# A fused convolution and sparse-expert block: moving small selection work, and transposing by image half

## The chip, the cores and the metric

The kernel runs on one core of one Trainium2 chip, in one launch. The time is device microseconds of that core; each value quoted for a kernel is the median of several runs. A separate execution is profiled and gives the trace.

## The reference

```python
x = x + conv_block(ln_c(x))     # ln_c: layer norm over the 64 channels of a pixel
t = to_tokens(x)                # [8, 16384, 64]
t = t + experts(ln_t(t))        # ln_t: layer norm of a token
x = from_tokens(t)

def conv_block(x):              # x: [8, 64, 128, 128] fp32
    xn = groupnorm(x, 8 groups) * gn_w + gn_b
    h = relu(w1 @ xn + b1)                      # 1x1 convolutions, 64 -> 64
    return x + w2 @ h + b2

def experts(x):                 # 32 experts, each takes its 8 best tokens of 16384
    logits = x @ gate_w.T + gate_b
    vals, idx = top_k(softmax(logits, over tokens), 8)
    pooled = sum over k of x[idx_k] * vals_k
    out = w2[e] @ [gelu(w1[e] @ [pooled, 1]), 1]
    return scatter_add(idx, out * vals)
```

## The kernel before

A batch (image) lies in SBUF as 128 partitions (two image halves of 64 channels) by 8192 pixels. It is cut into eight units `u` of 1024 columns. Two batches are resident (`xs`, `us`, two buffers each).

Iteration `it` works on three batches at once. For batch `b = it` it runs the convolutions, unit by unit: `conv1` (L350, TensorE), `relu` (L622, ScalarE), `conv2` (L361, TensorE), and `x1` (L784, VectorE), which adds `xs`, to which POOL has already added the normalized input (`add`, L1129). The next unit's `conv1` writes the banks `cv` that `x1` has just read. From the finished unit come `tokens` (transposes, copied by ScalarE in `token_copy` and stored by SP in `store`), `logits` (copied in `logits_copy`), and sums and sums of squares for the tokens' layer norm. For batch `n = it + 1` it computes the channel layer norm: sums (`x_sums`), `mean`, centering ("C" jobs), squares and their sums (`xc_square_sums`), `rstd`, scaling ("S" jobs with a group-norm sum). For batch `t = it - 1` it scales the logits ("L" jobs) and takes the top 8 of each of four pieces of 2048 positions (`top`, L848: a maximum and an index search over 1024 columns each), with an exponential and its sum on ScalarE (`explog`).

The pieces' winners become 32 candidates a row (`candidates`, L857), which one matrix product brings together ("M" job); `merge_pixels` and `merge_values` (L870, L892) take the final eight from them in many operations of a few hundred columns or fewer, with two small exponentials on ScalarE between (`merge_exps`, L682). This merge is for batch `m = it - 2`, in slots 2 and 3.

Everything is ordered by hand. Each engine runs its own queue in program order; a "slot" `s` is unit `s` of an iteration, and the dictionaries at L46 to L59 say at which place `(s, 0)` to `(s, 3)` of a slot a job stands. A job is: TensorE spreads 32-row statistics over 128 partitions into the two banks `bc` (`spread_stat`, L412), then VectorE uses them (`use_spread`, L760), then the banks are free for the next one. Unit 0 of each batch is done in `boundary`, together with the group norm (`group_norm`, L807), the last unit's tokens and the layer norm of the finished batch (`ln2_variance`, L833, `ln2_rstd`, L839). `boundary` also holds the top 8 of the fourth piece and the candidates. POOL's adds of units 6 and 7 wait for the group norm's bias.

In the last iteration there is no next batch; `spread_pixels` (L515), `diagonals` and `equal_pixels` compare the chosen pixel numbers of two batches, a pair in each of slots 5, 6 and 7, and `token_norm` normalizes the gathered rows. Then come the last batch's selection, the experts, and 16 indirect scatters.

The eight PSUM banks are `bc` (2), `cv` (2), `pt` (tokens), `lgp` (logits), `st1` and `st2` (sums).

Of the kernel before, what the change touches and what calls it, by code (L numbers as in the profile page):

```python
# [8 lines left out]
ALU = mybir.AluOpType  # L9
# [13 lines left out]
NCH = 2 * NU  # L23
# [26 lines left out]
M_JOB, LAST_M_JOB = (2, 3), (5, 0)  # L50


SUMSQ_AT = {(2, 1): (0,), (3, 0): (1,), (4, 0): (2,), (4, 1): (3,)}
# [3 lines left out]
TOP_AT = {3: 0, 5: 1, 6: 2}  # L57
LAST_TOP_AT = {1: 0, 2: 1, 3: 2, 4: 3}
LATE_ADDS = (6, 7)  # L59
PAIR_AT, NORM_AT = (5, 6, 7), (5, 6, 7)  # L60


def jobs_of(it):

    p1, tl, m = it + 1 < NB, 1 <= it <= NB, it - 2
    jobs = {}
    if p1:
        jobs.update({at: ("C", k) for at, k in C_JOBS.items()})
        jobs.update({at: ("S", k) for at, k in S_JOBS.items()})
    if tl:  # L70
        jobs.update({at: ("L", k) for at, k in (L_JOBS if p1 else LAST_L_JOBS).items()})
    if 0 <= m < NB - 2:
        jobs[M_JOB] = ("M", m)
    if it >= NB - 1:
        jobs[LAST_M_JOB] = ("M", it - 1)
    return jobs
# [9 lines left out]
def mk_metaformer_kernel(nc, x, gn_w, gn_b, w1T, b1, w2T, b2, gateT, gate_b, e_w1, e_w2, *outs):  # L86
    ctx = ExitStack()
    with ctx:
# [100 lines left out]
        pt, lgp, st1, st2 = banks("pt"), banks("lgp"), banks("st1"), banks("st2")  # L189
# [91 lines left out]
        def _(sp):  # L281
# [34 lines left out]
            def store(b, u):  # L316
                sp.wait_ge(tok_done, NCH * b + 2 * u + 2)
# [21 lines left out]
        def _(pe):  # L339
# [72 lines left out]
            def spread_stat(it, at):  # L412
# [18 lines left out]
                if kind == "M":  # L431
                    pe.wait_ge(cnd4_ready, k + 1)
                    pe.matmul(mrg_p, fold[:].rearrange("p g e -> p (g e)"), cnd4[:].rearrange("p r c -> p (r c)"),
# [15 lines left out]
            def boundary(it, par):  # L449
# [17 lines left out]
                if last >= 0:  # L467
                    x1_square_sums(last, NG - 1)
# [8 lines left out]
            def iteration(it, par, p1, p2):  # L477
                b, n = it, it + 1
                for s in range(0 if not p2 else 1, NU):
                    if p2:  # L480
                        conv1(b, par, s)
                        tokens(b, par, s - 1, 0)
                    spread_stat(it, (s, 0))
                    if p2:
                        logits(b, par, s - 1)
# [7 lines left out]
                    spread_stat(it, (s, 1))  # L493
                    if p2 and not p1 and s in PAIR_AT:
                        spread_pixels(PAIR_AT.index(s))
                    if p2:
                        conv2(b, s)
                        tokens(b, par, s - 1, 1)
                    spread_stat(it, (s, 2))
                    if p1:  # L500
                        for m in SUMSQ_AT.get((s, 1), ()):
# [13 lines left out]
            def spread_pixels(p):  # L515

                pe.wait_ge(diag_ready, p + 1)
                pe.wait_ge(bc_used, job_count(7, "M", 6) if p < 3 else job_count(8, "M", 7))
# [23 lines left out]
            pe.wait_ge(tok_done, NCH * NB)  # L542
# [67 lines left out]
        def _(act):  # L610
# [18 lines left out]
            def token_copy(b, u, sl):  # L629
                j = NCH * b + 2 * u + sl  # L630
                act.wait_ge(t_done, j + 1)
                wait(act, stored[u % 2], 16 * ((NU * b + u) // 2))
                nc.scalar.activation(tok[u % 2][:, :, 4 * sl:4 * sl + 4].rearrange("p h t c -> p t h c"),  # L633
                                     pt[:].rearrange("p (t h c) -> p t h c", t=4, h=2), ACT.Copy).then_inc(tok_done, 1)

            def logits_copy(b, u):
# [6 lines left out]
                nc.scalar.activation(lg[:, col:col + CH], lgp[:], ACT.Copy).then_inc(lcopy_done, 1)  # L643
# [44 lines left out]
            def boundary(it, par):  # L688
# [5 lines left out]
                if last >= 0:  # L694
                    token_copy(last, NU - 1, 0)
                    square_x1(last, 1 - par, NU - 1)
                    logits_copy(last, NU - 1)
                    token_copy(last, NU - 1, 1)
                if b < NB:
                    relu(b, par, 0)  # L700
                if last >= 0:
                    ln2_mean_square(last)
                    ln2_rsqrt(last)
                if 0 <= m < NB - 2:
                    explog(m, PIECES - 1)

            def iteration(it, par, p1, p2):
                b, n, t, m = it, it + 1, it - 1, it - 2
                tops = TOP_AT if p1 else LAST_TOP_AT
                for s in range(0 if not p2 else 1, NU):  # L710
                    if p2:
                        relu(b, par, s)
                        token_copy(b, s - 1, 0)
                    square_stat(it, (s, 0))
                    if p2:
                        logits_copy(b, s - 1)
                    square_stat(it, (s, 1))
                    if p2:
                        token_copy(b, s - 1, 1)
                        square_x1(b, par, s - 1)  # L720
                    square_stat(it, (s, 2))
                    if p1 and s == 4:
# [4 lines left out]
                        nc.scalar.activation(y0[:], lnv[:], ACT.Exp, scale=-0.5).then_inc(y0_ready, 1)  # L727
                    square_stat(it, (s, 3))
                    if t >= 0 and s in tops:
                        explog(t, tops[s])  # L730
                    if s == 3 and 0 <= m < NB - 2:
                        merge_exps(m)
                    if it == NB - 1 and s == 6:
                        merge_exps(t)
# [24 lines left out]
        def _(dve):  # L759
# [88 lines left out]
            def top(t, i):  # L848
# [4 lines left out]
                link(nc.vector.max(cnd[:, K * i:K * i + K], piece(t, i)))  # L853
                link(nc.vector.max_index(top_i[:, K * i:K * i + K], cnd[:, K * i:K * i + K], piece(t, i)))  # L854
# [335 lines left out]
```

## Time and profile before

| | |
|---|---|
| median of 3 runs | 765.37 us (764.79 to 770.71) |
| the profiled execution | 758.62 us, span 756.9 us |
| mean granted TensorE clock | 0.901 |
| TensorE matmul busy | 568.5 us, 75% |
| VectorE busy | 494.7 us, 65% |
| ScalarE busy | 428.0 us, 57% |
| GpSimd (POOL) busy | 185.1 us, 24% |

Busy time is how long an engine had an instruction in work, matmuls by a modelled end, so it is not a share of peak. The granted clock is a share of 2.4 GHz; it has two levels, 1.2 and 2.4 GHz. The span runs from the first to the last instruction. In the trace rows below, an "idle before" with a name in square brackets is how long the engine waited and for which instruction; PEld is TensorE's loading of weights. One row stands for several like instructions in a row (x4, x8, x16); a start is that of the first.

### The profile page before, as it was taken

The page shows a single profiled execution, that of the slowest core. Times are in us where ns is not written, and L with a number is a line of the kernel's source. Part 1 is how long each engine was busy: PE and PEld are TensorE (multiplying, and loading weights), DVE is VectorE, ACT ScalarE, POOL GpSimd, SP SyncE. Part 2 cuts the span into 40 slices and gives each one's busy share as a digit, 9 for nine tenths or more (in the row PEclk, how much of TensorE's full clock was granted, in tenths as well). Part 3 has the DMA queues.
Part 4 walks back from the last instruction along what each step waited for, and adds up shares of the span by engine and source line. Part 5 has one row for each costly group of instructions (what it writes and reads, how often), then busy time and mean ns, then how long its engine had stood idle before and what let it go on. Part 6 is the DMA issues. An engine that isn't in the chain of part 4 may idle for free.

```text
span 756.9 us, 14016 instructions
## 1 busy us (share of the span) xinstructions
PE 568.5 (75%) x5630; PEld 285.5 (38%) x5630; DVE 494.7 (65%) x919; ACT 428.0 (57%) x658; POOL 185.1 (24%) x110
## 2 busy tenths in 40 slices
PE   2544998898788878887888788878987867651682
PEld 0212344444344334443444344434443323230382
DVE  2344456668688768876887677778776876468320
ACT  0234587677857685768576856685768464222200
POOL 1026007203320332033204320342033700010025
PEclk9999999999999999999999999899999899775555
DMA  9930044634334333333333333333111295010000
GB/s 204 178 68 1 29 140 119 182 106 126 112 112 113 112 112 113 112 112 112 113 112 113 112 112 113 112 113 112 57 56 57 75 206 133 29 59 0 4 8 22
DMA packets 35428, 73.38 MB, mean 97 GB/s; under 512 B 12292, under 2 KB 14372, under 8 KB 31268
## 3 DMA queue, kind: packets, MB, share of 16 engines
q1 hardware_dynamic: 34340, 71.44, 34.6%
q0 software_dynamic: 1024, 1.05, 0.6%
q8 instruction: 45, 0.74, 0.4%
q14 instruction: 19, 0.16, 0.1%
HBM read 38.40 MB, written 34.08 MB: 96 GB/s over the span
## 4 chain that ended last, share of the span: by engine, by line
PE 42%; DVE 32%; issue 14%; ACT 6%; DMA 2%; POOL 1%; SPq 1%; ACTq 0%; DVEq 0%; POOLq 0%
PE st L346 9%; DVE xs L788 7%; PE bc L445 7%; PE lgp L383 6%; DVE top_i L854 6%; PE pt L373 5%; DVE cnd L853 5%; PE cv L357 5%; PE cv L365 4%; DVE us L778 3%; DVE us L780 3%; ACT hid L627 2%; DMA xs<-in_x 2%; ACT junk L666 2%; DVE lg L776 2%
## 5 line engine op out<-in xcount | busy, mean ns | idle before, releaser
L1135 POOL TENSOR_TENSOR xs<-xs,us 128x1024 f32<-128x1024 f32 x64 | 150.3, 2370 | 438.1 <-DVE gsum L780 354.9
L659 ACT ACTIVATE sqc<-us 128x1024 f32<-128x1024 f32 x64 | 67.5, 1054 | 78.9 <-DVE us L778 74.0
L373 PEld LDWEIGHTS pt<-ident,xs 128*128 128x128 f32 x512 | 68.6, 196 | 101.9 <-issue 100.5
L788 DVE SCALAR_TENSOR_TENSOR xs<-cv,vecs,xs 128x1024 f32<-128x1024 f32 x64 | 81.9, 1280 | 35.2 <-PE cv L365 35.0
L778 DVE TENSOR_TENSOR us<-xs,bc 128x1024 f32<-128x1024 f32 x64 | 77.9, 1217 | 39.6 <-PE bc L445 39.6
L633 ACT ACTIVATE tok<-pt 128x512 f32<-128x512 f32 x128 | 75.4, 589 | 47.6 <-PE pt L373 47.5
L445 PE MATMUL bc<-rstd_s,spread 32*128 32x256 f32 x384 | 54.2, 363 | 58.0 <-DVE gsum L780 32.1
L780 DVE CUSTOM_DVE_ANT_0 us<-us,bc 128x1024 f32<-128x1024 f32 x64 | 77.9, 1217 | 29.4 <-PE bc L445 29.4
L373 PE MATMUL pt<-ident,xs 128*128 128x128 f32 x512 | 94.7, 310 | 1.0 <-DVE xs L788 0.8
L346 PE MATMUL st<-xs,stat_w 128*32 128x256 f32 x1024 | 76.2, 426 | 16.1 <-DMA xs<-in_x 16.1
L666 ACT ACTIVATE junk<-us 128x1024 bf16<-128x1024 f32 x64 | 67.6, 1056 | 30.6 <-DVE gsum L780 30.6
L357 PE MATMUL cv<-us,w1n 64*64 64x512 f32 x512 | 72.1, 634 | 16.6 <-DVE xs L788 16.6
L627 ACT ACTIVATE hid<-cv,b1n 128x1024 f32<-128x1024 f32 x64 | 70.7, 1105 | 22.8 <-PE cv L357 22.2
L365 PE MATMUL cv<-hid,w2bd 64*64 64x512 f32 x512 | 72.7, 639 | 12.6 <-ACT hid L627 12.6
L383 PE MATMUL lgp<-xs,gcen 128*32 128x256 f32 x1024 | 76.3, 420 | 0.0
L648 ACT ACTIVATE sqx<-xs 128x1024 f32<-128x1024 f32 x64 | 67.3, 1051 | 0.0
L445 PEld LDWEIGHTS bc<-rstd_s,spread 32*128 32x128 f32 x384 | 32.9, 210 | 86.2 <-DVE gsum L780 41.4
L671 ACT ACTIVATE lg<-lg,nmax 128x1024 f32<-128x1024 f32 x32 | 36.6, 1145 | 50.0 <-DVE nmax L855 50.0
L346 PEld LDWEIGHTS st<-xs,stat_w 128*32 128x32 f32 x1024 | 34.4, 121 | 51.1 <-issue 24.3
L776 DVE TENSOR_TENSOR lg<-lg,bc 128x1024 f32<-128x1024 f32 x32 | 39.0, 1218 | 13.9 <-PE bc L445 12.6
L445 PE MATMUL bc<-mean_s,spread 32*128 32x256 f32 x256 | 34.7, 351 | 17.1 <-DVE mean_s L795 10.5
L346 PE MATMUL st<-sqc,stat_w 128*32 128x256 f32 x512 | 41.2, 448 | 1.8 <-ACT sqc L659 1.8
(181 smaller groups left out, 609.0 us busy)
## 6 DMA issues: line engine op xcount, KB each, us to landing
xs<-in_x SPq DMA_DIRECT2D x64, 512.0 KB, 6.4
out_rows<-tok SPq DMA_DIRECT2D x64, 512.0 KB, 2.8
us<-in_e_w SPq DMA_DIRECT2D x4, 520.0 KB
xs<-in_e_w SPq DMA_DIRECT2D x8, 256.0 KB
sqc<-out_rows,idx_all POOLq DMA_INDIRECT x16, 2.5
out_rows<-sqc,idx_all POOLq DMA_INDIRECT x16, 2.1
vecs<-in_b SPq DMA_DIRECT2D x4, 0.2 KB, 13.1
gate_bias<-in_gate_b SPq DMA_DIRECT2D x4, 0.1 KB, 11.4
```

What stands on the lines that cost most here:

```text
L346: mm = pe.matmul(dst[32 * c:32 * c + 32], stat_w[:, q, :], src[:, col:col + SUB], start=first and m == 0 and sub == 0, stop=True, skip_gro ...
L357: mm = pe.matmul(cv[C * sl:C * sl + C, CH * h:CH * h + CH], w1n[par][r, r], half_chunk(us[par], u, h, sl), start=True, stop=True)
L365: mm = pe.matmul(cv[C * h:C * h + C, CH * sl:CH * sl + CH], w2bd[r, r], hid[r, CH * h:CH * h + CH], start=True, stop=True)
L373: mm = pe.transpose(pt[:, P * k:P * k + P], unit(xs[par], u)[:, 4 * sl + k:UN:8], ident[:])
L383: mm = pe.matmul(lgp[NE * c:NE * c + NE, SUB * sl:SUB * sl + SUB], gcen[:, NE * h:NE * h + NE], xs[par][:, col:col + SUB], start=True, sto ...
L445: mm = pe.matmul(bc[:, CH * sl + SUB * i:CH * sl + SUB * i + SUB], weights, stat[32 * c:32 * c + 32, :], start=True, stop=True)
L627: nc.scalar.activation(hid[:], cv[:], ACT.Relu, bias=b1n[:, par:par + 1]).then_inc(h_done, 1)
L666: nc.scalar.activation(junk[:], unit(us[n % 2], k), ACT.Square, accum_out=gsq[:, k:k + 1]).then_inc(usq_done, 1)
L778: ins = nc.vector.tensor_tensor(unit(us[n % 2], k), unit(xs[n % 2], k), bc[:], ALU.subtract)
L780: ins = nc.vector.tensor_tensor_reduce(unit(us[n % 2], k), unit(us[n % 2], k), bc[:], 1.0, 0.0, ALU.mult, ALU.add, gsum[:, k:k + 1])
L788: nc.vector.scalar_tensor_tensor(out=xu, in0=cv[:], scalar=vecs[:, 3:4], in1=xu, op0=ALU.add, op1=ALU.add).then_inc(x1_done, 1)
L1135: nc.gpsimd.tensor_tensor(xu, xu, su, ALU.add).then_inc(s_done, 1)
```

## The change

Five things change together.

1. The selection of batch `t` runs in one iteration: maxima at `(s, 0)` in slots 2, 3, 5, 6, index searches behind `x1` of the same slots, candidates in slot 7, the M job at `(7, 2)`, and the merge's small operations in the following `boundary`, in place of the fourth piece's `top`.
2. The transposes of a unit are 16 of 64 partitions by a 64x64 identity instead of 8 of 128 partitions. The first half's go to one bank and the second half's to the other, in one group ahead of the first spread; one ScalarE copy of 128x1024 takes both. The first bank is also that of the logits, so `logits` moves behind the token copy and `conv2`.
3. Sums of squares move: all stand ahead of `conv2` but the first. ScalarE squares x1 and copies the logits later in the slot.
4. `ln2_variance` writes its intermediate to PSUM, not to SBUF.
5. POOL's adds of units 6 and 7 wait for `x1` of unit 1.

The last iteration is rearranged alike (pairs in slots 4, 5, 6).

```diff
-SUMSQ_AT = {(2, 1): (0,), (3, 0): (1,), (4, 0): (2,), (4, 1): (3,)}
+SUMSQ_AT = {(2, 2): (0,), (3, 0): (1,), (4, 0): (2,), (4, 1): (3,)}
-M_JOB, LAST_M_JOB = (2, 3), (5, 0)
+M_JOB, LAST_M_JOB = (7, 2), (6, 2)
-TOP_AT = {3: 0, 5: 1, 6: 2}
-LAST_TOP_AT = {1: 0, 2: 1, 3: 2, 4: 3}
+TOP_AT = {2: 0, 3: 1, 5: 2, 6: 3}
+LAST_TOP_AT = {2: 0, 3: 1, 4: 2, 5: 3}
-PAIR_AT, NORM_AT = (5, 6, 7), (5, 6, 7)
+PAIR_AT, NORM_AT = (4, 5, 6), (4, 5, 6)
...
-        pt, lgp, st1, st2 = banks("pt"), banks("lgp"), banks("st1"), banks("st2")
+        tl, st1, st2 = banks("tl", 2), banks("st1"), banks("st2")
+        lgp, pt = tl[:, 0:CH], tl[:, CH:2 * CH]
...
-            def tokens(b, par, u, sl):
+            def tokens(b, par, u):
                 pe.wait_ge(x1_done, NU * b + u + 1)
-                wait(pe, tok_done, NCH * b + 2 * u + sl)
-                for k in range(4):
-                    mm = pe.transpose(pt[:, P * k:P * k + P], unit(xs[par], u)[:, 4 * sl + k:UN:8], ident[:])
+                wait(pe, tok_done, NU * b + u)
+                wait(pe, lcopy_done, NU * b + u)
+                for k in range(8):
+                    for h in range(HALVES):
+                        r = slice(C * h, C * h + C)
+                        mm = pe.transpose(tl[:, CH * h + C * k:CH * h + C * k + C], unit(xs[par], u)[r, k:UN:8], ident[r, r])
                 mm.then_inc(t_done, 1)
...
             def logits(b, par, u):
-                pe.wait_ge(x1_done, NU * b + u + 1)
-                wait(pe, lcopy_done, NU * b + u)
+                pe.wait_ge(tok_done, NU * b + u + 1)
...
# TensorE, a slot
                     if p2:
                         conv1(b, par, s)
-                        tokens(b, par, s - 1, 0)
+                        tokens(b, par, s - 1)
                     spread_stat(it, (s, 0))
-                    if p2:
-                        logits(b, par, s - 1)
...
                     spread_stat(it, (s, 1))
+                    if p1:
+                        for m in SUMSQ_AT.get((s, 1), ()):
+                            xc_square_sums(n, m)
...
                         conv2(b, s)
-                        tokens(b, par, s - 1, 1)
+                        logits(b, par, s - 1)
                     spread_stat(it, (s, 2))
...
# TensorE, boundary
-                    tokens(last, 1 - par, NU - 1, 0)
-                    logits(last, 1 - par, NU - 1)
+                    tokens(last, 1 - par, NU - 1)
                     x1_sums(last, 1 - par, NG - 1)
-                    tokens(last, 1 - par, NU - 1, 1)
...
                     conv1(b, par, 0)
                 if last >= 0:
+                    logits(last, 1 - par, NU - 1)
                     x1_square_sums(last, NG - 1)
...
# ScalarE, a slot
                         relu(b, par, s)
-                        token_copy(b, s - 1, 0)
+                    if t >= 0 and s - 1 in tops:
+                        explog(t, tops[s - 1])
+                    if p2:
+                        token_copy(b, s - 1)
                     square_stat(it, (s, 0))
-                    if p2:
-                        logits_copy(b, s - 1)
                     square_stat(it, (s, 1))
...
+                    if p2:
+                        square_x1(b, par, s - 1)
+                        logits_copy(b, s - 1)
                     square_stat(it, (s, 2))
...
# VectorE, boundary
-                if 0 <= m < NB - 2:
-                    top(m, PIECES - 1)
+                if m >= 0:
+                    link3 = merge_pixels(it - 1, m)
                 if last >= 0:
                     link2 = Steps(dve, ln2_steps, LN2_STEPS * last)
                     ln2_variance(last, link2)
...
                     ln2_rstd(last, link2)
-                if 0 <= m < NB - 2:
-                    candidates(m)
+                if m >= 0:
+                    merge_values(m, link3)
# VectorE, a slot
                     use_spread(it, (s, 0))
+                    if t >= 0 and s in tops:
+                        top_values(t, tops[s])
+                    if t >= 0 and s == (7 if p1 else 6):
+                        candidates(t)
                     use_spread(it, (s, 1))
                     if p2:
                         x1(b, par, s)
-                    use_spread(it, (s, 2))
                     if p1 and s == 1:
                         mean(n)
                     if p1 and s == 4:
                         rstd(n)
...
+                    use_spread(it, (s, 2))
+                    if t >= 0 and s in tops:
+                        top_places(t, tops[s])
                     use_spread(it, (s, 3))
...
# ln2_variance
-                link(nc.vector.scalar_tensor_tensor(out=v2[:], in0=st2[:, SUB:2 * SUB], scalar=EPS, in1=ta[:],
+                link(nc.vector.scalar_tensor_tensor(out=st2[:, SUB:2 * SUB], in0=st2[:, SUB:2 * SUB], scalar=EPS, in1=ta[:],
                                                     op0=ALU.add, op1=ALU.subtract))
-                nc.vector.tensor_scalar(v2[:], v2[:], EPS, None, ALU.max).then_inc(var2_ready, 1)
+                nc.vector.tensor_scalar(v2[:], st2[:, SUB:2 * SUB], EPS, None, ALU.max).then_inc(var2_ready, 1)
# POOL, units 6 and 7
-                    pool.wait_ge(w1n_ready, 2 * (n + 1))
+                    pool.wait_ge(x1_done, NU * n + 2)
```

## Rows read from the trace of the kernel before

**Rows 1.** Windows: stretch, length, busy us of five engines, clock, DMA share, GB/s.
```profile
142.59:213.15 70.56, 60.73 (x668) 29.85 (x660) 53.09 (x81) 50.63 (x77) 18.82 (x8) 0.98 0.42 120
213.15:288.32 75.17, 62.88 (x667) 30.65 (x662) 57.87 (x103) 52.55 (x81) 18.82 (x8) 0.95 0.40 113
...
592.31:661.84 69.53, 49.88 (x399) 20.61 (x400) 45.15 (x97) 31.80 (x51) 11.51 (x12) 0.85 0.49 113
```

**Rows 2.** Timeline of TensorE in slot 3: start, us, operation.
```profile
231.32 1.09 PE L357 MATMUL cv<-us,w1n 64*64 64x512 f32 x8
232.34 0.71 PE L373 MATMUL pt<-ident,xs 128*128 128x128 f32 x4
232.98 0.50 PE L445 MATMUL bc<-mean_s,spread 32*128 32x256 f32 x4
233.41 1.07 PE L383 MATMUL lgp<-xs,gcen 128*32 128x256 f32 x16
234.30 1.05 PE L346 MATMUL st<-sqx,stat_w 128*32 128x256 f32 x16
235.16 1.05 PE L346 MATMUL st<-sqc,stat_w 128*32 128x256 f32 x16
...
236.57 1.09 PE L365 MATMUL cv<-hid,w2bd 64*64 64x512 f32 x8
...
239.16 1.09 PE L357 MATMUL cv<-us,w1n 64*64 64x512 f32 x8 [0.43 <-DVE xs L788]
```

**Rows 3.** The same timeline: `conv1` of the other slots, and the group-norm product.
```profile
214.47 1.09 PE L357 MATMUL cv<-us,w1n 64*64 64x512 f32 x8 [0.67 <-DVE xs L788]
...
222.56 1.09 PE L357 MATMUL cv<-us,w1n 64*64 64x512 f32 x8
...
251.61 1.12 PE L357 MATMUL cv<-us,w1n 64*64 64x512 f32 x8
...
259.76 1.09 PE L357 MATMUL cv<-us,w1n 64*64 64x512 f32 x8
...
268.58 1.09 PE L357 MATMUL cv<-us,w1n 64*64 64x512 f32 x8 [0.34 <-DVE xs L788]
...
277.89 0.38 PE L457 MATMUL bc<-gs,gsel 128*128 128x2 f32 x2 [1.51 <-DVE gs L812]
...
289.65 1.09 PE L357 MATMUL cv<-us,w1n 64*64 64x512 f32 x8 [0.67 <-DVE xs L788]
```

**Rows 4.** The same timeline: the stalled spread of slot 4.
```profile
246.61 0.51 PE L445 MATMUL bc<-rstd_s,spread 32*128 32x256 f32 x4 [2.56 <-DVE us L778]
```

**Rows 5.** Timeline of VectorE in slot 4: an operation of `merge_values`.
```profile
244.59 0.17 DVE L895 TENSOR_TENSOR djunk<-dexp,mrg 128x16 f32<-128x16 f32 x1 [1.71 <-ACT dexp L685]
```

**Rows 6.** Groups by line: busy us, mean ns of one, idle before them and its releasers.
```profile
L788 DVE SCALAR_TENSOR_TENSOR xs<-cv,vecs,xs 128x1024 f32<-128x1024 f32 x64 | 81.9, 1280 | 35.2 <-PE cv L365 35.0
L778 DVE TENSOR_TENSOR us<-xs,bc 128x1024 f32<-128x1024 f32 x64 | 77.9, 1217 | 39.6 <-PE bc L445 39.6
L633 ACT ACTIVATE tok<-pt 128x512 f32<-128x512 f32 x128 | 75.4, 589 | 47.6 <-PE pt L373 47.5
L627 ACT ACTIVATE hid<-cv,b1n 128x1024 f32<-128x1024 f32 x64 | 70.7, 1105 | 22.8 <-PE cv L357 22.2
L373 PEld LDWEIGHTS pt<-ident,xs 128*128 128x128 f32 x512 | 68.6, 196 | 101.9 <-issue 100.5 <-DVE xs L788 1.0
L853 DVE MAX8 cnd<-lg 128x8 f32<-128x1024 f32 x32 | 39.2, 1224 | 0.1
L671 ACT ACTIVATE lg<-lg,nmax 128x1024 f32<-128x1024 f32 x32 | 36.6, 1145 | 50.0 <-DVE nmax L855 50.0
```

**Rows 7.** Timeline of TensorE in the last iteration: the pixel products of slots 5 and 6.
```profile
634.91 1.12 PE L520 MATMUL bc<-xs,gsel 128*128 128x512 f32 x2
...
645.79 2.07 PE L520 MATMUL bc<-xs,gsel 128*128 128x512 f32 x2 [3.73 <-DVE xs L985]
```

**Rows 8.** Line 837, the variance's clamp: ns of one, least/median/most; first and last start.
```profile
L837 DVE TENSOR_SCALAR lnv<-lnv x8: 295/1966/2329, 140.5 to 668.4; 128x256 f32<-128x256 f32 x8
```

More of the change, by code:

```diff
@@ L432, in spread_stat @@
                     pe.wait_ge(cnd4_ready, k + 1)
+                    if it == NB - 1:
+                        pe.wait_ge(eq_ready, 3)
                     pe.matmul(mrg_p, fold[:].rearrange("p g e -> p (g e)"), cnd4[:].rearrange("p r c -> p (r c)"),
@@ L497, in iteration @@
                         conv2(b, s)
-                        tokens(b, par, s - 1, 1)
+                        logits(b, par, s - 1)
                     spread_stat(it, (s, 2))
                     if p1:
-                        for m in SUMSQ_AT.get((s, 1), ()):
+                        for m in SUMSQ_AT.get((s, 2), ()):
                             xc_square_sums(n, m)
@@ L541, in _ @@
             pe.wait_ge(ew_in, 16 * 13)
-            pe.wait_ge(tok_done, NCH * NB)
+            pe.wait_ge(tok_done, NU * NB)
             for h in range(HALVES):
@@ L694, in boundary @@
                 if last >= 0:
-                    token_copy(last, NU - 1, 0)
+                    token_copy(last, NU - 1)
                     square_x1(last, 1 - par, NU - 1)
-                    logits_copy(last, NU - 1)
-                    token_copy(last, NU - 1, 1)
                 if b < NB:
@@ L701, in boundary @@
                 if last >= 0:
+                    logits_copy(last, NU - 1)
                     ln2_mean_square(last)
                     ln2_rsqrt(last)
-                if 0 <= m < NB - 2:
-                    explog(m, PIECES - 1)
+                if m >= 0:
+                    merge_exps(m)
             def iteration(it, par, p1, p2):
@@ L727, in iteration @@
                         nc.scalar.activation(y0[:], lnv[:], ACT.Exp, scale=-0.5).then_inc(y0_ready, 1)
+                    if p2:
+                        square_x1(b, par, s - 1)
+                        logits_copy(b, s - 1)
+                    square_stat(it, (s, 2))
                     square_stat(it, (s, 3))
[L729 to L734, printed above, removed]
                     if p2 and not p1 and s == NORM_AT[1]:
@@ L846, in ln2_rstd, with top_values @@
                 assert link.n == LN2_STEPS, link.n
-            def top(t, i):
+            def top_values(t, i):
                 link = Steps(dve, top_steps, TOP_STEPS * t + 2 * i)
@@ L930, in iteration @@
                         rstd(n)
-                    use_spread(it, (s, 3))
-                    if t >= 0 and s in tops:
-                        top(t, tops[s])
-                    if s == 2 and 0 <= m < NB - 2:
-                        link3 = merge_pixels(it, m)
-                    if s == 3 and 0 <= m < NB - 2:
-                        merge_values(m, link3)
+                    if not p1 and s in PAIR_AT:
+                        equal_pixels(PAIR_AT.index(s))
+                    use_spread(it, (s, 2))
+                    if t >= 0 and s in tops:
+                        top_places(t, tops[s])
+                    use_spread(it, (s, 3))
                     if p2 and not p1:
@@ L940, in iteration @@
                             nc.vector.memset(ones[:], 1.0)
-                        if s == 4:
-                            candidates(t)
-                        if s == 5:
-                            link3 = merge_pixels(it, t)
-                        if s == 6:
-                            merge_values(t, link3)
                         if s in NORM_AT:
                             token_norm(0, 0, 6, (NORM_AT.index(s),))
-                        if s in PAIR_AT:
-                            equal_pixels(PAIR_AT.index(s))
                         if s + 1 in PAIR_AT:
@@ L1048, in _ @@
             for i in range(PIECES):
-                top(7, i)
+                top_values(7, i)
+                top_places(7, i)
             candidates(7)
```

30 lines of the change are left out of this document (11 added, 19 removed).

## The prediction

> **What bounds the kernel now.** I cut the run into stretches from one batch's first `x1` to the next [rows 1]. Five steady iterations, 213.15 to 592.31, take 75.8 us each; in the one that starts at 213.15 VectorE is busy 57.9, ScalarE 52.6 and TensorE 62.9 us (a span that is not its peak), so no engine is full and waits set the pace. The iteration before it, which has no merge, no late fourth piece and no candidates, took 70.56 us: the small selection work costs about 5 us where it stands.
>
> TensorE's timeline tells where. In slot 3 its groups follow one another without a gap [rows 2], so their spacing is their price: `conv1` 1.02, four transposes 0.64, a spread 0.43, `logits` 0.89, a sum group 0.86, `conv2` 1.02 us. From one `conv1` to the next, slots 1 to 6 last 8.09, 8.76, 7.84, 12.45, 8.15 and 8.82 us; from the last `conv1` to the group-norm product 9.31, and from there to the next iteration's second `conv1` 11.76 (214.47 to 289.65, 75.18 in all) [rows 2, 3]. The outlier is slot 4: the spread at 246.61 stood idle for 2.56 us, for VectorE's subtraction that should have freed the `bc` banks. VectorE had queued a whole top-8 (maximum and index search) and the end of a merge ahead of it, and the merge waited another 1.71 us for ScalarE, whose small exponentials sat behind the 1.15 us one [rows 4 to 6]. Behind that stall TensorE lost its clock (0.95 of full speed on average over the iteration [rows 1]), which makes slot 4 longer still.
>
> **The change, part by part.** Let t be the time of a unit's sixteen transposes. I walk a steady iteration in each engine's new order, with durations of one instruction [rows 2, 6] and 0.1 us for a hand-over between engines. These sums are estimates.
>
> *Transposes.* Two groups of four cost 2 x 0.64 = 1.28 us. Now 16 instructions load 64x128 and stream 64 columns. Four of the old ones, each loading 128 and streaming 128 columns, take 0.64, so 0.16 each, and with half the streaming 0.12 if loading and streaming weigh alike. If the two row halves run side by side, t is 8 x 0.12 = 0.96; one after the other, 16 x 0.12 = 1.92. Lower end, if only the streamed columns count and halves overlap: 8 x 0.08 = 0.64. I take 0.95, because other packed tiles overlap here: `conv1` streams eight times 512 columns in 1.02 us in quarters of the array [rows 2], a full-array product of twice 512 columns takes 1.12 [rows 7]. ScalarE's copy of 128x1024 should cost what its PSUM-read ReLU of that shape costs, 1.10, against 2 x 0.59 before [rows 6]: nothing won. The banks are the hidden price: transposes of a unit now also wait for the copy of the previous unit's logits, and logits for the token copy.
>
> *Slots 2 and 3.* The order is `conv1`, transposes, spread, VectorE job, maximum, job, `x1`, next `conv1`: 1.02 + t + 0.43 + 1.22 + 1.22 + 1.22 + 1.28 and hand-overs of about 0.1 = 6.5 + t = 7.45 us each. Index searches fall after `x1`, beside TensorE work, and the merge is gone: gains of 1.3 and 0.4.
>
> *Slot 4.* No piece is searched and no merge stands here, but the last sum of squares now precedes `conv2` and needs the seventh square, which ScalarE reaches after ReLU, exponential and copy, at 6.5 us (its queue is 2.2 us late from slot 3: 2.2 + 1.1 + 1.2 + 1.0 + 1.0). Then sum 0.9, `conv2` 1.0, `logits` 0.9, spread 0.45: 9.8, a gain of 2.65, and TensorE stands idle 1.7 us.
>
> *Slots 5 and 6.* VectorE enters slot 5 with the reciprocal root and a logits job, 3.15 us; then maximum, job, `x1`, job, about 1.25 each, and the last spread 0.5: 8.65 (a loss of 0.5). Slot 6: ScalarE's ReLU begins at 3.3, behind the third square; ReLU, exponential and copy end at 6.6, then `logits` and a spread: 8.0 (gain 0.8).
>
> *Slot 7.* Transposes wait for the logits copy until 2.35; S6, the candidates with their wait for the last exponential (5.75), S7, `x1`, the merge's two copies and the last square bring the group-norm product to 9.7 (loss 0.4). The POOL queue's two late adds now start behind the second `x1`, and are needed five slots later: nothing; its gathers, queued behind them, find their indices earlier. SP's store waits for one copy of a unit instead of two, no later than before: nothing.
>
> *Boundary.* The whole old top-8 goes, 14 small operations of the merge come at about 0.2 us each, some 2.8 us either way, and both lie beside TensorE's own chain to `conv2`: product 0.4, t with a 0.4 wait, sums 0.9, bias product 0.2, `conv1` 1.0, `logits` 0.9, three sum groups 2.7 make 7.5 us to `conv2`, and 2.5 to the next `conv1`; the old way took 11.76 with a throttled stretch in it, so I add 1.0: 10.95 (gain 0.8). The clamp of the variance lasted 1.97 us at the median and 0.295 at the least, where POOL was quiet [rows 8]; with a PSUM source I give it 0.42, but in the sum above `conv2`, not the clamp, sets the start of `x1`: I count 0.3.
>
> A rule bears on that. The Trainium skill ("SBUF — State Buffer", Who interferes with whom) says that VectorE in a two-port mode and GpSimd take a shared port pair in turn, each blocking the other wholly. By it the clamp gives back 1.55 us seven times, 11 us, if it set the end; the trace agrees with the 1.97 against 0.295, but not that the end waits for it.
>
> *Slot 1.* `mean` now precedes the second logits job and waits for the last sum of x, which stands behind `logits`: the first spread of the next batch moves from 4.6 to 5.0 us behind `conv2`. With the merge's last four operations inside `ln2`'s shadow: 8.4 (loss 0.3).
>
> Sum: 8.4 + 7.45 + 7.45 + 9.8 + 8.65 + 8.0 + 9.7 + 10.95 = 70.4 against 75.2. I add 1.4 for one more stretch at the lower clock: 71.8. Over five iterations 5 x 71.8 = 359 against 379.2: -20.2. The 70.56 one gains the work it lacked: +1.2. The first iteration has no selection: 0.
>
> *The last iteration* took 69.5 us from `x1` to `x1` [rows 1]. If its four slots without a pixel product take 8.2 us each, like the steady ones, the three with one take 12.2 each. There `conv2` waits behind the product, which waits for VectorE's diagonals: 3.73 us idle at 645.79 [rows 7]. The merge leaves these slots (2.8 us and a tail of four operations, 0.8) and index searches (1.5) stay in two of them. From `x1` through equality, search, normalization and diagonals to the next product, `conv2` and `x1` I count 9.8, 9.8 and, without a following pair, 7.5: -9.5; the merge product's wait for the third equality gives back 1: -8.5. The rest, 95 us, keeps its chain: 0.
>
> Total -27.5 us. The profiled execution took 758.62 us (span 756.9); the median of the runs is 765.37, 6.75 above. So 731 by the profiled one, and 738 by the median, which I forecast.
>
> **The rivals.**
> *Slower: the row halves do not overlap.* Then t = 1.92, one us more, in about six places of eight iterations: +48, so 738 + 48 = 786. It turns the gain into a loss when t passes 0.95 + 27.5/48 = 1.5. Against it: the quarters of `conv1` [rows 2]. For it: nothing in this trace shows a transpose in a tile.
> The Trainium skill ("TensorE: Matmul & The Clock Gate", LDWEIGHTS) has load time go by columns, not by rows. The trace agrees, 196 ns for 128x128 [rows 6]: by it sixteen loads of half the rows cost sixteen full loads.
>
> *The gain goes to new waits and the clock.* The walk leaves TensorE idle 2.2 us in slot 1, 1.7 in slot 4 and 2.0 in slot 5; 2.56 us of idling went before a slower clock in the old slot 4. If each is followed by a stretch like it, 1.6 us apiece, an iteration is 75 us: 738 + 6 x 3.2 = 757; range 748 to 764.
>
> *A larger gain.* If the long stall's end keeps the clock at its upper level and t is 0.64, an iteration is 68.5: 738 - 20 = 718.
>
> *It does nothing*, since the bound is TensorE's own work: the gapless slot 3 speaks for it, slot 4 against it: 765.
>
> **How the numbers follow.** Forecast 730 to 748: 0.50. New waits and clock: 0.23. Larger gain: 0.11. Slower: 0.11. Nothing: 0.05. Less than 1% (7.7 us) can't be told from no change. Faster takes the forecast, the larger gain and nearly two thirds of the second case: 0.75; same: the rest of that and the last: 0.14; slower 0.11. The range leaves out most of the slower case and the far end of the larger gain: 720 to 765.
>
> **What would show it.** Right: a unit's 16 transposes span about 1 us; from `x1` to `x1` of two batches 70 to 73 us; the slot-4 spread has no 2.6 us gap and TensorE waits instead for ScalarE's square; the clamp takes 0.4 us; last iteration near 61. Wrong: transposes at 1.5 us or more; gaps of 2 us in slots 1 and 5 with a granted clock below 0.93; ScalarE's token copies waited for by `logits` in most slots.

## The result, and the profile after

The changed kernel takes 742.26 us (median of four runs, 740.17 to 742.73); the kernel before took 765.08 beside it (762.92 to 770.71). The ratio is 0.9686, interval 0.9631 to 0.9741: 22.8 us less. The forecast was 738. Some executions of a kernel are slower as a whole, at a lower granted clock; the ratios leave them out, and the profile of `old_clamp` below is of such a one.

The profiled execution took 742.05 us, span 740.3. The windows from `x1` to `x1`, columns as in [rows 1]: a steady iteration, the last one, and the first.

```profile
363.75:435.42 71.67, 62.32 (x730) 29.73 (x729) 56.00 (x102) 51.51 (x73) 18.78 (x8) 0.93 0.43 119
...
578.90:644.67 65.77, 46.48 (x444) 18.64 (x448) 40.14 (x71) 30.79 (x41) 16.20 (x14) 0.84 0.52 120
79.50:146.81 67.31, 59.19 (x712) 27.73 (x710) 35.23 (x55) 47.21 (x63) 18.77 (x8) 0.95 0.41 116
```

The five steady iterations took 359.65 us together instead of 379.16, 3.9 less on the average. In the one shown TensorE is busy 0.6 us less than in the second row of [rows 1] and VectorE 1.9, 1.55 of it in the clamp: most of the 3.5 us between these two is waits. The last iteration lost 3.8 us, the first grew by 3.6, and the second, 70.56 us before, took 72.44.

TensorE's timeline in slots 3 and 4, answering to [rows 2] and [rows 4]:

```profile
382.45 1.09 PE L355 MATMUL cv<-us,w1n 64*64 64x512 f32 x8
383.47 1.10 PE L374 MATMUL tl<-ident,xs 64*128 64x64 f32 x16
384.50 0.50 PE L447 MATMUL bc<-mean_s,spread 32*128 32x256 f32 x4
...
396.17 1.07 PE L344 MATMUL st<-sqc,stat_w 128*32 128x256 f32 x16 [1.01 <-ACT sqc L659]
```

Sixteen transposes occupy 383.47 to 384.50, 1.03 us, where two groups of four took 1.28. The stalled spread is gone, and TensorE waits in slot 4 for ScalarE's square instead.

In the boundary, VectorE's timeline shows small operations of the merge at their bare length, and then idle time before `x1`; the last row answers to the clamp of [rows 8]:

```profile
430.52 0.17 DVE L875 CAST best<-fpos 128x8 f32<-128x8 uint32 x1
430.73 0.16 DVE L876 TENSOR_TENSOR gbm<-best,gate_bias 128x1 f32<-128x1 f32 x1
...
433.56 0.42 DVE L831 TENSOR_SCALAR lnv<-st 128x256 f32<-128x256 f32 x1
435.42 1.28 DVE L782 SCALAR_TENSOR_TENSOR xs<-cv,vecs,xs 128x1024 f32<-128x1024 f32 x1 [1.44 <-PE cv L363]
```

One thing that the prediction has nowhere stands in slot 3 of the last iteration. TensorE first, then ScalarE, VectorE, POOL. Where a bracket has `issue` or `remote`, the profile names no instruction that ended the wait:

```profile
593.88 1.10 PE L374 MATMUL tl<-ident,xs 64*128 64x64 f32 x16
594.91 1.07 PE L344 MATMUL st<-sqx,stat_w 128*32 128x256 f32 x16
595.91 1.09 PE L363 MATMUL cv<-hid,w2bd 64*64 64x512 f32 x8
599.94 1.51 PE L383 MATMUL tl<-xs,gcen 128*32 128x256 f32 x13 [2.95 <-ACT tok L634]
...
608.86 1.99 PE L355 MATMUL cv<-us,w1n 64*64 64x512 f32 x8 [6.09 <-DVE xs L782]
```
```profile
598.87 1.02 ACT L634 ACTIVATE tok<-tl 128x1024 f32<-128x1024 f32 x1 [2.61 <-remote]
606.05 1.06 ACT L648 ACTIVATE sqx<-xs 128x1024 f32<-128x1024 f32 x1 [6.17 <-remote]
...
607.52 1.28 DVE L782 SCALAR_TENSOR_TENSOR xs<-cv,vecs,xs 128x1024 f32<-128x1024 f32 x1 [12.10 <-issue]
...
590.35 1.12 POOL L1118 DMA_INDIRECT sqc<-out_rows,idx_all  x1 [0.17 <-issue]
...
604.26 0.95 POOL L1118 DMA_INDIRECT sqc<-out_rows,idx_all  x1 [0.30 <-issue]
```

The transposes end by 595 and the copy that waits for them starts at 598.87; `conv2` ends by 597 and `x1` starts at 607.52, which had nothing else to wait for. By TensorE's records the work is done, and the news of it comes 4 to 11 us late, while POOL issues twelve gathers (590.35 to 605.2). Slot 3 takes 16.0 us.

### The profile page after: what moved, and what is told of

The parts are those of the page before. It is cut to its first block, busy times and chain, and to the rows that moved or that the text cites. A ratio compares the mean times of both kernels' runs of the same rounds, so it can differ in the third digit from the quotient of the medians.

```text
span 740.3 us, 14809 instructions
## 1 busy us (share of the span) xinstructions
PE 564.1 (76%) x6142; PEld 276.7 (37%) x6142; DVE 480.8 (65%) x919; ACT 422.0 (57%) x594; POOL 184.8 (25%) x110
## 4 chain that ended last, share of the span: by engine, by line
PE 42%; DVE 27%; issue 15%; ACT 11%; DMA 3%; POOL 1%; SPq 1%; ACTq 0%; another core or an unknown queue 0%; DVEq 0%; POOLq 0%
PE st L344 11%; PE bc L447 6%; PE tl L374 6%; DVE us L774 6%; PE cv L355 6%; DVE xs L782 5%; PE cv L363 4%; PE tl L383 3%; DVE cnd L847 3%; DVE lg L770 3%; DVE us L772 2%; DMA xs<-in_x 2%; DVE top_i L852 2%; ACT lg L671 2%; ACT sqc L659 2%
## 5 line engine op out<-in xcount | busy, mean ns | idle before, releaser
L772 DVE TENSOR_TENSOR us<-xs,bc 128x1024 f32<-128x1024 f32 x64 | 78.1, 1221 | 40.2 <-PE bc L447 39.7
L629 ACT ACTIVATE hid<-cv,b1n 128x1024 f32<-128x1024 f32 x64 | 70.8, 1106 | 53.9 <-PE cv L355 53.9
L344 PE MATMUL st<-xs,stat_w 128*32 128x256 f32 x1024 | 86.4, 472 | 16.8 <-DMA xs<-in_x 16.8
L355 PE MATMUL cv<-us,w1n 64*64 64x512 f32 x512 | 76.1, 667 | 13.7 <-DVE xs L782 12.4
L374 PEld LDWEIGHTS tl<-ident,xs 64*128 64x128 f32 x1024 | 62.1, 201 | 64.6 <-issue 63.3
L374 PE MATMUL tl<-ident,xs 64*128 64x64 f32 x1024 | 71.1, 287 | 15.3 <-ACT lg L643 15.2
L383 PE MATMUL tl<-xs,gcen 128*32 128x256 f32 x1024 | 73.0, 401 | 5.3 <-ACT tok L634 4.9
L634 ACT ACTIVATE tok<-tl 128x1024 f32<-128x1024 f32 x64 | 64.9, 1015 | 7.4 <-PE tl L374 4.8
L383 PEld LDWEIGHTS tl<-xs,gcen 128*32 128x32 f32 x1024 | 27.9, 112 | 74.3 <-issue 38.7
L447 PE MATMUL bc<-mean_s,spread 32*128 32x256 f32 x256 | 36.4, 365 | 23.1 <-DVE lg L770 13.7
L344 PEld LDWEIGHTS st<-xs,stat_w 128*32 128x32 f32 x1024 | 32.2, 127 | 52.8 <-issue 29.0
L643 ACT ACTIVATE lg<-tl 128x512 f32<-128x512 f32 x64 | 37.5, 585 | 18.9 <-PE tl L383 18.4
```

What stands on the lines that cost most here:

```text
L344: mm = pe.matmul(dst[32 * c:32 * c + 32], stat_w[:, q, :], src[:, col:col + SUB], start=first and m == 0 and sub == 0, stop=True, skip_gro ...
L355: mm = pe.matmul(cv[C * sl:C * sl + C, CH * h:CH * h + CH], w1n[par][r, r], half_chunk(us[par], u, h, sl), start=True, stop=True)
L374: mm = pe.transpose(tl[:, CH * h + C * k:CH * h + C * k + C], unit(xs[par], u)[r, k:UN:8], ident[r, r])
L383: mm = pe.matmul(lgp[NE * c:NE * c + NE, SUB * sl:SUB * sl + SUB], gcen[:, NE * h:NE * h + NE], xs[par][:, col:col + SUB], start=True, sto ...
L447: mm = pe.matmul(bc[:, CH * sl + SUB * i:CH * sl + SUB * i + SUB], weights, stat[32 * c:32 * c + 32, :], start=True, stop=True)
L629: nc.scalar.activation(hid[:], cv[:], ACT.Relu, bias=b1n[:, par:par + 1]).then_inc(h_done, 1)
```

## The experiments

All ratios are to the kernel before, run on the same chip. Its median was 756.0 us beside `sel_only`, `tok_only`, `full128` and `serial_halves`, 760.2 beside `after_again`, `weights_late`, `sumsq_late` and `old_clamp`, and 756.3 beside the other four, so times of different groups are compared by ratio. The edits are shown against the changed kernel; `...` marks lines left out.

**One half of the change each.** `sel_only` keeps the old transposes and banks, and has all the rest of the change, parts 3 to 5 too:

```diff
-        tl, st1, st2 = banks("tl", 2), banks("st1"), banks("st2")
+        pt, lgp, st1, st2 = banks("pt"), banks("lgp"), banks("st1"), banks("st2")
...
-                        tokens(b, par, s - 1)
+                        tokens(b, par, s - 1, 0)
                     spread_stat(it, (s, 0))
+                    if p2:
+                        logits(b, par, s - 1)
```

> The kernel before with the selection work spread as in the changed kernel, and the transposes, their two copies and the banks as they were. Theory A (the selection work carries the gain): the long wait of slot 4 and the merge leave the iteration, a steady iteration takes 72 to 73 us from x1 to x1 against 75.8, the whole about 746 (ratio 0.975). Rival B (the transposes and the one copy carry it): 758 or more, a steady iteration 75 us. Rival C (the parts need each other): 765 or above.

`tok_only` has the new transposes, banks, copy and place of `logits`, and the selection work, the other sums of squares, the clamp and the wait of the late adds as they were:

```diff
-M_JOB, LAST_M_JOB = (7, 2), (6, 2)
+M_JOB, LAST_M_JOB = (2, 3), (5, 0)
...
-TOP_AT = {2: 0, 3: 1, 5: 2, 6: 3}
+TOP_AT = {3: 0, 5: 1, 6: 2}
```

> The kernel before with the transposes per row half into two banks with one copy, and logits behind conv2; the selection work stays where it was. Theory A: 1.28 us of transposes a unit become 1.05, everything else of slot 4's wait stays: a steady iteration 74.5 to 76 us, the whole 757 to 766. Rival B: 745 or less. Rival C (the bank chain transposes, token copy, logits, logits copy alone makes it slower): above 772.

Measured: `sel_only` 728.56 us, 0.9616 (0.9572 to 0.9661); `tok_only` 765.12, 1.0132 (1.0082 to 1.0183). A window of each, and a row of TensorE's timeline of `tok_only`:

```profile
286.71:358.45 71.74, 63.76 (x666) 30.93 (x665) 55.63 (x103) 52.07 (x83) 18.83 (x8) 0.93 0.42 118
```
```profile
289.37:364.27 74.90, 61.78 (x730) 29.26 (x729) 57.26 (x103) 52.17 (x74) 18.85 (x8) 0.95 0.41 113
364.27:445.19 80.92, 68.57 (x730) 30.97 (x729) 56.78 (x102) 53.13 (x74) 18.81 (x8) 0.85 0.38 105
```
```profile
322.79 0.51 PE L447 MATMUL bc<-rstd_s,spread 32*128 32x256 f32 x4 [2.77 <-DVE us L772]
```

For `sel_only` theory A holds, and more: the change without its transposes carries the whole gain (0.9616 where 0.975 was expected). How much of that is the moved selection and how much the new wait of the late adds, `adds_old` shows below. For `tok_only` theory A fell and rival C came: scaled to this chip, A ended at 1.001 and C began at 1.009. The old stall of slot 4 stays, [2.77 <-DVE us L772]. Where the loss lies is not shown. The profiled execution is the fastest of its four (761.02 us), and its five steady iterations take 380.7 us together against 379.2: 74.9, 74.9, 80.9, 76.4 and 73.5 us, where the kernel before has one of 78.1 and four of 75.1 to 75.6. That the bank chain causes the long ones is not shown either.

**The transposes.** `full128`; its one copy also reorders as it reads:

```diff
                 for k in range(8):
-                    for h in range(HALVES):
-                        r = slice(C * h, C * h + C)
-                        mm = pe.transpose(tl[:, CH * h + C * k:CH * h + C * k + C], unit(xs[par], u)[r, k:UN:8], ident[r, r])
+                    mm = pe.transpose(tl[:, P * k:P * k + P], unit(xs[par], u)[:, k:UN:8], ident[:])
```

> The changed kernel with eight transposes of all 128 rows and the whole identity instead of sixteen of 64 rows, into the same two banks; the one copy reorders as it reads. Theory: a transpose of four in the old kernel stepped 0.113 us, so eight take 1.0 to 1.1 us and with them the unit costs what the sixteen cost (1.02 to 1.10): the time is within 0.4% of the changed kernel's 742. Rival A (halving is what makes them cheap): eight take 1.28 us, 0.2 more in 50 units or so: 752. Rival B (the reordering copy costs ScalarE more than 1.1 us, at 1.2 to 1.3): 745 to 750.

`serial_halves` only exchanges the two loops (`for h` outside, `for k` inside).

> The changed kernel with the sixteen transposes issued all of the upper half first and then all of the lower half. Theory (neighbours in different row halves run side by side, neighbours in the same half do not): the unit's transposes take 1.8 to 1.9 us instead of 1.05, and with 0.8 us in six slots of eight iterations on TensorE's path the time is 765 to 785. Rival (a 64-row transpose costs half of one of 128 rows by itself, order does not matter): 1.05 us a unit, 742.

Measured: `full128` 729.15 us, 0.9644 (0.9608 to 0.9680); `serial_halves` 755.95, 1.0023 (0.9986 to 1.0059). The timeline of `full128`, then of `serial_halves`; the start of the next row is the end of the transposes:

```profile
381.60 1.16 PE L372 MATMUL tl<-ident,xs 128*128 128x128 f32 x8
382.69 0.50 PE L445 MATMUL bc<-mean_s,spread 32*128 32x256 f32 x4
```
```profile
393.67 1.59 PE L374 MATMUL tl<-ident,xs 64*128 64x64 f32 x16
395.20 0.51 PE L447 MATMUL bc<-mean_s,spread 32*128 32x256 f32 x4
```

`full128` does not have the long slot 3 of the last iteration (57.3 us for that iteration instead of 65.8). These 8.5 us are 1.1% of the time, and by its ratio it is 0.4% ahead of the changed kernel as first measured and 1.3% ahead of the same kernel measured again below; the stall is looked into there. Eight full transposes take 1.09 us, sixteen halves in turn 1.03, sixteen halves one side after the other 1.53. So neighbours in different row halves do run together, and I had their price apart too high (1.53, not 1.9). Those 0.44 us a unit more than `full128` cost 26.8 us in all (755.95 less 729.15). Halving brings 0.06 us over full transposes. What the unit gained on 1.28 us lies in joining two groups of four, not in halving. A load of 64 rows does last as long as one of 128 (200 and 196 ns), and yet sixteen such loads do not make the group longer than eight.

**The last iteration.** `after_again` is the changed kernel once more.

> The changed kernel itself once more, on the chip of the edits beside it. Its first profile had 8 us in slot 3 of the last iteration in which TensorE's instructions were issued but their completions came late. Theory A (it happens each time, from gathers and expert weights moving together): x1 to x1 over the last iteration is again above 64 us and the ratio to the kernel before is 0.969. Theory B (an accident of that execution): 57 to 60 us, as the kernel with full transposes had, with gathers and weight loads at the same offsets.

`weights_late`:

```diff
-                    if it == NB - 1 and 2 <= s <= 5:
-                        load_weights(s - 2)
+                    if it == NB - 1 and 4 <= s <= 7:
+                        load_weights(s - 4)
```

> The changed kernel with the expert weights of the last iteration issued in slots 4 to 7 instead of 2 to 5. If their packets beside the gathers make the 8 us stall of slot 3: last iteration 57 to 60 us, the whole 6 to 8 us (1%) below the changed kernel. Rival (the stall is not theirs, or does not come each time): same within 0.4%; if the weights then come too late for the tail, 3 us or more slower.

Measured: 743.35 us, 0.9770 (0.9713 to 0.9827), and 739.65, 0.9721 (0.9642 to 0.9799), not to be told apart. The same kernel has come out at 0.9686 and at 0.9770, so a difference of less than 1% between kernels of different groups says little. Slot 3 of the last iteration took 16.22 us in the one and 16.19 in the other. In `weights_late` SP issues no weights until 599.4, and `x1` still waits:

```profile
605.17 1.28 DVE L782 SCALAR_TENSOR_TENSOR xs<-cv,vecs,xs 128x1024 f32<-128x1024 f32 x1 [12.30 <-issue]
...
599.37 0.47 SPq L309 DMA_DIRECT2D gbd<-in_e_w  x1
```

The stall comes in each of the profiles with this instruction order and these waits, and the weights are not its cause. `gathers_early` moves the other suspect:

```diff
             for n in range(NB):
                 for k in range(NU):
+                    if n == NB - 1 and k == LATE_ADDS[0]:
+                        for b in range(5):
+                            gather(b)
                     add(n, k)
-            for b in range(6):
-                gather(b)
+            gather(5)
```

> The changed kernel with the gathers of batches 0 to 4 ahead of the last batch's two late adds on the POOL queue, so that ten of the twelve run before the last iteration begins; only batch 5 stays behind the adds. Moving the expert weights left the 16.2 us slot 3 of the last iteration where it was, so my theory is now that the late completions of TensorE need the gathers beside it: slot 3 falls to 6 to 8 us, the last iteration from 66 to 57 to 60 us, the whole 6 to 9 us below the changed kernel (0.97 becomes 0.96). Rival A (the late completions come from TensorE's own code at that place): slot 3 stays at 16 us, same time. Rival B (the gathers take the stall with them): 8 us appear in slot 7 or at the boundary before the last iteration, same time.

Measured: 728.69 us, 0.9638 (0.9601 to 0.9674). Its windows, then TensorE's timeline in slot 3 of the last iteration:

```profile
364.35:436.00 71.65, 62.27 (x730) 29.72 (x729) 55.99 (x103) 51.53 (x73) 18.77 (x8) 0.93 0.43 118
577.83:630.52 52.69, 42.89 (x444) 17.57 (x448) 40.15 (x71) 30.58 (x41) 6.62 (x4) 0.94 0.61 143
```
```profile
594.83 1.09 PE L363 MATMUL cv<-hid,w2bd 64*64 64x512 f32 x8
596.15 1.07 PE L383 MATMUL tl<-xs,gcen 128*32 128x256 f32 x16 [0.23 <-ACT tok L634]
597.39 1.09 PE L355 MATMUL cv<-us,w1n 64*64 64x512 f32 x8 [0.16 <-DVE xs L782]
```

Slot 3 falls to 5.59 us, the last iteration to 52.7, and the stall turns up nowhere else. My theory holds as far as it went; by the ratio the gain is 0.5% on the first measurement of the changed kernel, which is within the noise, and 1.3% on the second. Gathers alone do not make the stall: `sel_only` and `full128` began their twelve 13.5 to 27.4 and 11.5 to 25.4 us into the last iteration, the changed kernel 11.5 to 25.4, and had 6.07 and 5.65 us in slot 3.

Nor is it bound to slot 3. In the profile of `old_clamp`, the next experiment, the twelve gathers are issued from 593.36 to 608.2, 2.4 us before the last iteration and on; its slot 3 takes 5.59 us and its slot 1 14.71. TensorE, then VectorE, whose operation needs that spread and starts 8 us after its end, then the last of the gathers:

```profile
600.08 0.80 PE L447 MATMUL bc<-rstd_s,spread 32*128 32x256 f32 x4
...
608.99 1.22 DVE L770 TENSOR_TENSOR lg<-lg,bc 128x1024 f32<-128x1024 f32 x1 [9.12 <-remote]
...
607.26 0.94 POOL L1118 DMA_INDIRECT sqc<-out_rows,idx_all  x1 [0.30 <-issue]
```

`adds_old` differs from it only by the clamp and issues its gathers at the same place (596.90 to 611.75, also from 2.4 us before the last iteration), with 7.09 us in slot 1 and no such wait. What has to come together stays open.

**The clamp and the late adds.** `old_clamp` undoes both small edits, `adds_old` only the second:

```diff
-                link(nc.vector.scalar_tensor_tensor(out=st2[:, SUB:2 * SUB], in0=st2[:, SUB:2 * SUB], scalar=EPS, in1=ta[:],
+                link(nc.vector.scalar_tensor_tensor(out=v2[:], in0=st2[:, SUB:2 * SUB], scalar=EPS, in1=ta[:],
...
-                    pool.wait_ge(x1_done, NU * n + 2)
+                    pool.wait_ge(w1n_ready, 2 * (n + 1))
```

> The changed kernel with the clamp's source in SBUF again and the two late adds waiting for the folded weights, as before. My theory (conv2, not the clamp, sets the boundary's x1, which VectorE waits 1.44 us for): the clamp goes from 0.42 to about 2 us and takes that idle time, 0 to +0.3 us an iteration, and in the last iteration the gathers start earlier and the 2.9 us wait for their rows goes: between -4 and +2 us in all. Rival (the clamp's time counts in full): 1.55 us in seven boundaries, +11 us (1.5%).

> The changed kernel with only the wait of the two late adds put back as before, so that they start behind the folded weights, in the boundary; the clamp still reads PSUM. Theory (in the kernel with both edits undone a cast and a small addition of the merge lasted 2.29 and 2.28 us beside the two adds, 0.17 and 0.16 without them; the clamp does not matter): 4.2 us in each of six boundaries less 1.4 us of idle time, the ratio to the kernel before is 0.99, as with both undone. Rival (the clamp's PSUM source protects): 0.97 to 0.975.

Measured: `old_clamp` 756.1 us, 0.9933 (0.9888 to 0.9978); `adds_old` 751.11, 0.9898 (0.9854 to 0.9941). My theory on `old_clamp` fell: it lost 1.6% to the changed kernel beside it. But its rival was wrong too, since the clamp there lasted 0.29 us at the median. Between the two kernels nothing can be told, so the clamp's source in PSUM shows no gain of its own: with POOL elsewhere the clamp lasts 0.42 us from PSUM and 0.29 from SBUF. `adds_old` names the place, VectorE's timeline and then POOL's:

```profile
366.98 0.29 DVE L874 FIND_INDEX8 fpos<-best,cval 128x8 uint32<-128x128 f32 x1
367.30 2.27 DVE L875 CAST best<-fpos 128x8 f32<-128x8 uint32 x1
369.61 2.27 DVE L876 TENSOR_TENSOR gbm<-best,gate_bias 128x1 f32<-128x1 f32 x1
371.91 0.17 DVE L877 TENSOR_TENSOR mine<-best,kmask 128x16 f32<-128x16 f32 x1
...
374.44 1.27 DVE L782 SCALAR_TENSOR_TENSOR xs<-cv,vecs,xs 128x1024 f32<-128x1024 f32 x1
...
367.17 4.69 POOL L1128 TENSOR_TENSOR xs<-xs,us 128x1024 f32<-128x1024 f32 x2 [9.81 <-DVE b1n L825]
```

A conversion of eight numbers a row and an addition of one last 2.27 us each, the second until POOL's two adds end (367.17 + 4.69 = 371.86); without the adds they lasted 0.17 and 0.16. `x1` has no idle time left, TensorE waits 2.67 us for it, and what follows runs near half clock (granted 0.56 from 379 to 384 us). The steady five iterations take 378.9 us, as much as before the change, though slot 3 of the last one takes 5.6 here: the change without this one wait gains 1%, and not 3.

The Trainium skill ("SBUF — State Buffer", Who interferes with whom) says that VectorE and GpSimd share one port pair as an exclusive lock, so that one blocks the other fully while it holds it, and that a cast can take the pair and an operation with two SBUF inputs contends with a GpSimd one that reads SBUF. The trace agrees: 2.27 us against 0.17 and 0.16, each about as long as one of the adds (4.69 us for two).

**TensorE's wait in slot 4.** `sumsq_late`:

```diff
-SUMSQ_AT = {(2, 2): (0,), (3, 0): (1,), (4, 0): (2,), (4, 1): (3,)}
+SUMSQ_AT = {(2, 2): (0,), (3, 0): (1,), (4, 0): (2,), (4, 2): (3,)}
```

> The changed kernel with the last sum of squares of x behind conv2 and logits of slot 4 instead of ahead of them. Theory: TensorE's 1.0 us wait for ScalarE's square in slot 4 ([1.01 <-ACT sqc]) goes and conv2 of slot 4 starts up to 1.9 us earlier; rstd of slot 4 comes 0.5 us later: -0.7 us in each of seven iterations, -5 us (0.7%). Rival (VectorE's rstd behind it sets slot 5, whichever way): 0 to +3 us.

Measured: 741.56 us, 0.9736 (0.9667 to 0.9805), not to be told from the changed kernel beside it. From one `x1` to the next, slot 4 went from 9.75 to 7.76 us, slot 5 from 7.02 to 10.04, and the last stretch, into the next batch, from 12.1 to 10.96. Iterations 3, 4 and 5 take 71.7 us as before; that iterations 2 to 6 come to 357.0 us instead of 359.65 lies in the second (71.75 for 72.83) and the sixth (70.16 for 71.80), and no row says why. So the rival holds: VectorE's timeline shows the wait one slot on, for the reciprocal root, where the changed kernel has none:

```profile
396.94 0.42 DVE L272 SCALAR_TENSOR_TENSOR tb<-st,y 128x256 f32<-128x256 f32 x1 [2.03 <-ACT y L723]
```

**Combinations.** `sel_gathers` is `sel_only` with the early gathers, `full_gathers_sumsq` is `full128` with them and the later sum of squares; the edits are those above.

> The selection work spread as in the changed kernel, the old transposes and banks, and the gathers of batches 0 to 4 ahead of the late adds. The kernel without the last edit had no late completions (last iteration 58.8 us) but VectorE waits for gathered rows in the pixel slots: 1 to 4 us less than it, ratio 0.957 to 0.961. If gathers before the last iteration cost their own stall there: 0.965 or more.

> The changed kernel with eight full transposes, the early gathers and the last sum of squares behind conv2. The full transposes gave 0.9644, the pixel slot of 14.3 us with its 2.9 us wait for rows should fall to 10.5, the sum of squares gave 0.5 us an iteration: ratio 0.955 to 0.960. If the bank chain outweighs it: 0.965, behind the kernel with the old transposes.

Measured: 725.4 us, 0.9607 (0.9568 to 0.9646), and 724.91, 0.9597 (0.9557 to 0.9637). Both are below the changed kernel's 0.9686; between them, and against `sel_only` (0.9616), nothing can be told. Leaving the transposes as they were gave as much as the whole change with its stall mended (0.9638).

## Why the prediction was right, and where it was not

*The time* came nearer than the working. The working gave 27.5 us less in the profiled execution, 731; it took 742.05, only 16.6 less. The median was forecast by adding the 6.75 us by which the profile before lay below its median. The profile after lies 0.2 below, and that made 11 us of error into 4: luck. The terms, forecast and measured in the two profiles: five steady iterations -20.2 and -19.5, the second +1.2 and +1.9, the first 0 and +3.6, the last -8.5 and -3.8, the rest 0 and +1.2.

*The steady iteration* was right: 71.8 us forecast, 71.67 measured. Slots 1 to 6, from one `conv1` to the next, were forecast at 8.4, 7.45, 7.45, 9.8, 8.65 and 8.0 us and measured 8.79, 8.57, 7.46, 9.76, 8.58 and 7.82; slot 7 9.7 and 9.13, the boundary 10.95 and 11.56. The 1.4 us for one more stretch at the lower clock was spent in slot 2, after 2.29 us of idling. The wait for ScalarE's square is where the walk put it, 1.01 us for 1.7.

*The transposes* were mis-sized by little, 0.95 for 1.03, for the right reason (halves overlap). The rival that they do not is refuted, and its price was overdrawn: 1.53 us instead of 1.92. The count of 48 places on the path was low: 0.44 us a unit cost 26.8, as much as 61 places. A part of it is the clock, which was granted at 0.880 in the profile of `serial_halves` and at 0.911 in that of `full128`. And halving, which the working took for the source of this gain, is not: full transposes in one group do as well.

*The late adds* are the step that failed in its reasoning: "The POOL queue's two late adds now start behind the second `x1`, and are needed five slots later: nothing". That asked who waits for them and not whom they hold up. With the merge in the boundary this one wait is worth 19.2 us in five iterations (378.88 against 359.65; 22 against `gathers_early` on the chip of `adds_old`). The sum came out right because the merge's operations were priced at 0.2 us, which holds only while POOL is quiet. I had weighed the port rule on the clamp, which the sum rightly gave next to nothing, and not on the moved merge.

*The last iteration*: -8.5 forecast, -3.8 measured. The pixel slots were forecast at 9.8, 9.8 and 7.5 and took 10.42, 10.28 and 7.83, against 12.05, 12.72 and 11.99. The other four were left at 8.2 us each, 32.8 in all; they took 5.16, 7.47, 15.99 and 8.62. Without the stall, in `gathers_early`, they take 5.16, 7.47, 5.59 and 6.65. So two terms were missing, some -8 us for slots that the selection leaves and +12 for the stall and what follows it. "Its gathers, queued behind them, find their indices earlier" named the queue and missed what it does: the first gather moved from 0.1 to 11.5 us of this iteration.

*The first iteration*: 0 forecast, +3.6 in this profile. The second profile of the same kernel has 64.43 us there, +0.7, at a granted clock of 1.00 instead of 0.95. Most of the 3.6 is the clock; no row says why it fell.

*By the rivals:* of "new waits and the clock" the waits came, 2.29 us at the end of slot 1 and 1.83 in slot 5, and the clock over the whole run fell from 0.901 to 0.882, but the steady iterations took 71.7 us and not 75. What the forecast had nowhere was the stall of the last iteration, 12 us, and the 8 us won there, which hid most of it.

## What to carry to other kernels

When small VectorE work is moved, look at what GpSimd does at the new place: here two tiny operations beside two large adds, and the clock behind them, cost as much as the steady iterations had gained. Price a moved queue item twice, for who waits for it and for what it then runs beside. Before splitting transposes by row half, join the full ones into one group: 1.09 us for eight, against 1.03 for the halves and 1.28 for two groups. A forecast from one profiled execution holds for such an execution; its distance to the median (6.75 us before, 0.2 after) is not a constant to be added.

## What the runs showed of the hardware

- TensorE's completions can arrive late. With gathers on the POOL queue beside it, slot 3 took 16.0, 16.22, 16.19 and 16.19 us in four profiles of kernels with that instruction order, and 5.6 to 6.1 in others with gathers at the same offsets; in `old_clamp`, with earlier gathers, it was slot 1, 14.71 us. That moving ten of the gathers ahead ends it is shown; what else it takes is open.
- Transposes: eight of 128 rows 1.09 us, sixteen of 64 rows in turn 1.03, not in turn 1.53. A load of 64 rows lasts 200 ns and one of 128 rows 196 ns.
- Tiny operations of VectorE from SBUF beside adds of POOL last as long as an add: 2.27 us instead of 0.17 and 0.16.
- Steady iterations came out at 71.6 to 71.8 us in six different kernels (the changed one, `gathers_early`, `sumsq_late`, `sel_only`, `sel_gathers`, `full_gathers_sumsq`), whatever was taken from a slot, each at a mean granted clock below 1 (0.93 to 0.98); other iterations of the same kernels took 69.3 to 70.8 or 71.9 to 74.0 us. A saving of half a microsecond seems to be given back there in waiting or clock. Why the same number returns was not tried.
